# A four-block transformer kernel: the last stage's weights centred on the chip, and two engines' attention loops written out

## The reference

```python
def _layernorm(x, g, b):
    m = jnp.mean(x, axis=-1, keepdims=True)
    v = jnp.mean(jnp.square(x - m), axis=-1, keepdims=True)
    return (x - m) * jax.lax.rsqrt(v + LN_EPS) * g + b
...
gate_scores = xf @ gate_W + gate_b
topk_scores, topk_idx = jax.lax.top_k(gate_scores, 2)
weights = jax.nn.softmax(topk_scores, axis=-1)
def expert(w1, bb1, gg1, bbe1, w2, bb2, gg2, bbe2):
    h = jax.nn.relu(_layernorm(xf @ w1 + bb1, gg1, bbe1))
    return _layernorm(h @ w2 + bb2, gg2, bbe2)
...
out = jnp.sum(weights[..., None] * exp_out, axis=1)
return (out + xf).reshape(B, N, D)
```

## Time and profile before

| | us |
|---|---|
| median of 3 runs | 2317.06 |
| lowest and highest | 2315.38, 2320.44 |
| the profiled execution | 2316.81 |
| its span | 2315.0 |

### The profile page before, as it was taken

The page is one execution under the profiler, slowest core; times in us unless marked ns, Lnnn a source line. Parts: engine busy times, 40 slices in busy tenths (PEclk is TensorE's granted clock), DMA queues, the critical chain, the costliest instruction groups (busy, mean ns, idle before and its releaser), DMA issues.

```text
span 2315.0 us, 55192 instructions
## 1 busy us (share of the span) xinstructions
PE 2190.0 (95%) x18512; PEld 1811.2 (78%) x18512; DVE 1749.1 (76%) x4736; ACT 1193.1 (52%) x2397; POOL 1230.9 (53%) x2200
## 2 busy tenths in 40 slices
PE   6999999999699999999969999999989999999997
PEld 5878778777588888888858888888777777777775
DVE  5888888887465665666569887788678888888885
ACT  4655555555233333233236666666566666666663
POOL 5667667676200000000057666666468888888886
PEclk9999999999799999999989999999999999999998
DMA  7412121211221222221042222222100000000000
GB/s 233 143 58 65 56 65 57 63 59 49 103 94 40 91 84 85 86 83 55 28 135 66 75 69 68 73 66 71 49 26 29 28 28 27 27 27 27 27 24 17
DMA packets 125389, 148.06 MB, mean 64 GB/s; under 512 B 13835, under 2 KB 117523, under 8 KB 122773
## 3 DMA queue, kind: packets, MB, share of 16 engines
q1 hardware_dynamic: 119060, 128.84, 17.4%
q0 software_dynamic: 6144, 16.79, 2.3%
...
## 4 chain that ended last, share of the span: by engine, by line
PE 71%; DVE 11%; POOL 8%; issue 5%; ACT 2%; DMA 1%; POOLq 0%; SPq 0%; DVEq 0%; ACTq 0%
PE ps L1201 11%; PE ps L1074 10%; PE ps L1215 8%; PE ps L1059 5%; PE ps L1139 5%; PE ps L1217 4%; PE ps L1013 4%; PE ps L1158 4%; PE ps L972 4%; DVE u2g L1275 3%; PE ps L925 3%; PE ps L1106 3%; PE ps L1030 2%; DVE h_st L1244 2%; PE ps L1007 2%
## 5 line engine op out<-in xcount | busy, mean ns | idle before, releaser
L1344 DVE TENSOR_REDUCE nmax<-ps 128x16 f32<-128x2048 f32 x128 | 293.0, 2289 | 51.4 <-PE ps L1030 51.4
L665 POOL COPY slot_in<-slot_all 128x1 int32 (+1 forms) x64 | 18.2, 284 | 566.9 <-DMA eo_d<-eo 566.9
L896 ACT ACTIVATE hid<-ps,b_in 128x512 f32<-128x512 f32 x192 | 132.4, 690 | 361.0 <-PE ps L1201 338.4
L834 ACT ACTIVATE prob_t<-ps 128x2048 f32<-128x2048 f32 x128 | 240.5, 1879 | 76.6 <-PE ps L1013 76.6
L1215 PE MATMUL ps<-w_hl,hid_hi 128*128 128x512 f32 x768 | 269.6, 394 | 0.0
L1201 PE MATMUL ps<-xgt_hi,w_hl 128*128 128x512 f32 x768 | 242.9, 392 | 1.5 <-DVE xgt_lo L1543 1.5
L972 PE MATMUL ps<-w2f,a_t 128*128 128x256 f32 x1024 | 243.3, 381 | 0.0
L972 PEld LDWEIGHTS ps<-w2f,a_t 128*128 128x128 f32 x1024 | 195.5, 191 | 27.4
L1217 PE MATMUL ps<-w_hl,hid_lo 128*128 128x256 f32 x768 | 214.9, 280 | 0.0
L748 ACT ACTIVATE z<-ps,h_rs 128x256 f32<-128x256 f32 x256 | 123.7, 563 | 164.6 <-POOL h_rs L620 164.6
L639 POOL TENSOR_TENSOR km_r<-qk,cst 128x512 fp32r<-128x512 f32 x128 | 133.4, 1042 | 119.1 <-ACT qk L824 118.8
...
## 6 DMA issues: line engine op xcount, KB each, us to landing
c_t<-in_ctx_in_dram SPq DMA_DIRECT2D x128, 128.0 KB
...
x_d<-x SPq DMA_DIRECT2D x128, 128.0 KB, 2.1
...
```

The lines of the kernel that those rows point to most:

```text
L834: nc.scalar.activation(prob_t[:].rearrange("p a k -> p (a k)"), scores.rearrange("p a k -> p (a k)"), ACT.Exp, scale=SOFT).then_inc(y["exp ...
L896: nc.scalar.activation(hid[:, fc % 2, :], ps[:, 4 + fc % 2, 0:G], ACT.Gelu, bias=b1_in[:, e.parity, fc:fc + 1]).then_inc(z["hid_done"].sem, 1)
L1344: nc.vector.tensor_reduce(nmax[:, b.parity, :, 0:4], scores.rearrange("p a (r k) -> p a r k", k=P), AX_X, ALU.max, negate=True).then_inc(y ...
```

## The change

Each expert's w1, w2 and b2 are centred on the chip: the mean over the output columns is taken off each row of the weights and off the bias, so that the results of both matmuls have mean zero. The first and the second normalisation then need no mean. GpSimd drops the last two instructions of h_rs and the last of the k group, z is an ACT.Copy with a scale and no bias, gw8 and be_in keep four columns and four rows, and one load goes. The statistics are still taken. The means and subtractions are ten new large instructions on VectorE, and the preparation now runs from step 7 to step 42 of the second attention, with at most one large instruction of VectorE at the end of a step; ScalarE's parts move with it. Finally both attentions are written out on VectorE and on ScalarE (span None).

```diff
@@ GpSimd, fstep
                     nc.gpsimd.tensor_tensor(k_rw[:], k_rs[:, 1, :], gw8[:, b.parity, 0:E1], ALU.mult).then_inc(st.sem, 1)
-                    pool.wait_ge(st.of(b), st.at(b, 3))
-                    nc.gpsimd.tensor_tensor(gw8[:, b.parity, E1:2 * E1], k_mv[:, :, 0], k_rw[:], ALU.mult).then_inc(st.sem, 1)
...
                     nc.gpsimd.tensor_tensor(h_rs[:, 1, :], h_rs[:, 0, :], neg_half.to_broadcast([P, E1]), ALU.pow).then_inc(st.sem, 1)
-                    pool.wait_ge(st.of(b), st.at(b, 2))
-                    nc.gpsimd.tensor_tensor(h_rs[:, 2, :], h_mv[:, :, 0], h_rs[:, 1, :], ALU.mult).then_inc(st.sem, 1)
-                    pool.wait_ge(st.of(b), st.at(b, 3))
-                    nc.gpsimd.tensor_tensor(h_rs[:, 3, :], h_rs[:, 2, :], neg_one.to_broadcast([P, E1]), ALU.mult).then_inc(st.sem, 1)
@@ ScalarE, fstep
-                        nc.scalar.activation(z1[:, b.parity, e, :], ps[:, 2 + e // 2, (e % 2) * D:(e % 2 + 1) * D], ACT.Identity,
-                                             scale=h_rs[:, 1, e:e + 1], bias=h_rs[:, 3, e:e + 1]).then_inc(f["z_act"].sem, 1)
+                        nc.scalar.activation(z1[:, b.parity, e, :], ps[:, 2 + e // 2, (e % 2) * D:(e % 2 + 1) * D], ACT.Copy,
+                                             scale=h_rs[:, 1, e:e + 1]).then_inc(f["z_act"].sem, 1)
@@ ScalarE, preparation: w1_hi now at LAST_SPLIT + 12 and + 13
-                        nc.scalar.activation(b2_hi[:], b2_raw[:], ACT.Copy).then_inc(s_fset, 1)
+                    if n == 1 and s.off == LAST_SPLIT + 28:
+                        act.wait_ge(s_fset2, 20)
+                        nc.scalar.activation(b2_hi[:], b2_raw[:], ACT.Copy).then_inc(s_fset, 1)
-                run_steps(act, B, LEAD, TAIL[n], WARM, step, SPAN)
+                run_steps(act, B, LEAD, TAIL[n], WARM, step, None)
@@ VectorE, preparation
+                    if n == 1 and s.off == LAST_SPLIT + 3:
+                        dve.wait_ge(s_fset2, 1)
+                        nc.vector.tensor_reduce(w1_mean[:, 0], w1f[:, 0], AX_X, ALU.add).then_inc(s_fset2, 1)
...
+                    if n == 1 and s.off == LAST_SPLIT + 8:
+                        dve.wait_ge(s_fset2, 5)
+                        nc.vector.tensor_tensor(w1f[:, 0], w1f[:, 0], w1_mean[:, 0].unsqueeze(2).to_broadcast([P, E1, D]), ALU.subtract)\
+                            .then_inc(s_fset2, 1)
...
+                    if n == 1 and s.off == LAST_SPLIT + 23:
+                        dve.wait_ge(s_fset2, 17)
+                        nc.vector.tensor_tensor(w2f[:, 0:2], w2f[:, 0:2], w2_mean[:, 0:2].unsqueeze(3).to_broadcast([P, 2, C, D]), ALU.subtract)\
+                            .then_inc(s_fset2, 1)
...
-                run_steps(dve, B, LEAD, TAIL[n], WARM, step, SPAN)
+                run_steps(dve, B, LEAD, TAIL[n], WARM, step, None)
```

More of the change, by code:

```diff
@@ L324, in flamingo_gated @@
         b2_raw = psb("b2_raw", [2, E1, D])
+        w1_mean = psb("w1_mean", [P, C, E1])
+        w2_mean = psb("w2_mean", [P, E1, C])
+        b2_mean = psb("b2_mean", [2, E1])
         b2_hi = psb("b2_hi", [2, E1, D], F32R)
@@ L355, in flamingo_gated @@
         h_mv = psb("h_mv", [P, E1, 2])
-        h_rs = psb("h_rs", [P, 4, E1])
+        h_rs = psb("h_rs", [P, 2, E1])
         s_set = sem("s_set")
@@ L461, in layer1_weights @@
                     sp.dma_start(dst[0:E1] if dst is be2_in else dst[:], src).then_inc(s_fw, 16)
-                sp.dma_start(be2_in[E1:2 * E1], g2_1[0]).then_inc(s_fw, 16)
             def attention_weights(n):
@@ new lines, in step @@
+                    if n == 1 and s.off == LAST_SPLIT + 2:
+                        nc.vector.tensor_tensor(w1f[:, 1], w1f[:, 1], w1_first[:, 1], ALU.subtract).then_inc(s_fset2, 1)
+                    if n == 1 and s.off == LAST_SPLIT + 3:
+                        dve.wait_ge(s_fset2, 1)
+                        nc.vector.tensor_reduce(w1_mean[:, 0], w1f[:, 0], AX_X, ALU.add).then_inc(s_fset2, 1)
+                    if n == 1 and s.off == LAST_SPLIT + 4:
+                        dve.wait_ge(s_fset2, 2)
+                        nc.vector.tensor_reduce(w1_mean[:, 1], w1f[:, 1], AX_X, ALU.add).then_inc(s_fset2, 1)
@@ L1502, in step @@
+                    if n == 1 and s.off == LAST_SPLIT + 10:
+                        nc.vector.tensor_tensor(w1f[:, 1], w1f[:, 1], w1_mean[:, 1].unsqueeze(2).to_broadcast([P, E1, D]), ALU.subtract)\
+                            .then_inc(s_fset2, 1)
+                    if n == 1 and s.off == LAST_SPLIT + 14:
+                        dve.wait_ge(s_fset, 2)
                         nc.vector.tensor_tensor(w1_lo[:, 0], w1f[:, 0], w1_hi[:, 0], ALU.subtract).then_inc(s_fset2, 1)
-                    if n == 1 and s.known and s.off == LAST_SPLIT + 4:
-                        dve.wait_ge(s_fset, 5)
+                    if n == 1 and s.off == LAST_SPLIT + 15:
+                        dve.wait_ge(s_fset, 4)
@@ new lines, in step @@
+                    if n == 1 and s.off == LAST_SPLIT + 18:
+                        nc.vector.tensor_reduce(w2_mean[:, 2:4], w2f[:, 2:4], AX_X, ALU.add).then_inc(s_fset2, 1)
+                    if n == 1 and s.off == LAST_SPLIT + 20:
+                        nc.vector.tensor_reduce(b2_mean[:], b2_raw[:], AX_X, ALU.add).then_inc(s_fset2, 1)
+                    if n == 1 and s.off == LAST_SPLIT + 21:
+                        dve.wait_ge(s_fset2, 15)
+                        nc.vector.tensor_scalar(w2_mean[:], w2_mean[:], 1.0 / D, None, ALU.mult).then_inc(s_fset2, 1)
+                        nc.vector.tensor_scalar(b2_mean[:], b2_mean[:], 1.0 / D, None, ALU.mult).then_inc(s_fset2, 1)
@@ new lines, in step @@
+                    if n == 1 and s.off == LAST_SPLIT + 27:
+                        nc.vector.tensor_tensor(b2_raw[:], b2_raw[:], b2_mean[:].unsqueeze(2).to_broadcast([2, E1, D]), ALU.subtract)\
+                            .then_inc(s_fset2, 1)
+                    if n == 1 and s.off == LAST_SPLIT + 29:
+                        nc.vector.tensor_scalar(g2_in[:], g2_in[:], g_t[:, 3:4], None, ALU.mult).then_inc(s_fset2, 1)
+                    if n == 1 and s.off == LAST_SPLIT + 31:
+                        dve.wait_ge(s_fset, 5)
@@ L1508, in step @@
                         nc.vector.tensor_tensor(b2_lo[:], b2_raw[:], b2_hi[:], ALU.subtract).then_inc(s_fset2, 1)
-                        nc.vector.tensor_scalar(be2_in[0:2 * E1], be2_in[0:2 * E1], be_sign, None, ALU.mult).then_inc(s_fset2, 1)
-                    if n == 1 and s.known and s.off == LAST_SPLIT + 6:
-                        dve.wait_ge(s_fset2, 9)
+                    if n == 1 and s.off == LAST_SPLIT + 33:
+                        dve.wait_ge(s_fset2, 22)
                         nc.vector.tensor_scalar(b2_lo[:], b2_lo[:], hilo_mask[:, 1:2], None, ALU.mult).then_inc(s_fset2, 1)
```

58 lines of the change are left out of this document (30 added, 28 removed).

## The result

| | us (the ratio has no unit) |
|---|---|
| changed kernel, median of 4 runs | 2291.45 |
| lowest and highest | 2290.61, 2291.59 |
| its profiled execution, span | 2291.34, 2289.4 |
| the kernel before, in the same comparison | 2317.36 |
| ratio, 95% interval | 0.9885 (0.9872 to 0.9897) |

I forecast 2297.0 and a range of 2291 to 2304. Scaled to the median of 2317.06 that the forecast started from, the ratio gives 2290.4, just outside the range. The mechanism in the last stage was right and the gain was forecast too small. Medians and ratios in this document are over undisturbed runs; two runs of the kernel before beside e1 to e4, 2401.8 and 3554.6 us at granted clocks of 0.90 and 0.56, are left out.

A forecast was written before the change was run, and what follows sets the result against it. The prediction took a ring of waits across four engines in the last stage as the bound. Its gains, 17.1 + 2.2 + 0.3 + 0.2 = 19.8 us, off 2316.8 gave 2297.0 us, range 2291 to 2304.

The forecast's parts named there:

- The ring: Last stage: waits from k_st through k_rs, frs, xf and TensorE back to k_st set the round, 9.56 to 9.28 us.
- the wait for z at L991: Last stage: TensorE's 0.19 us wait for z, forecast to be gone after the change.
- 0.28 x 61 = 17.1: Last stage: the removed k instruction (L582) saves 0.28 us in each of 61 rounds, 17.1 us.
- Two thirds of what is removed is worth nothing.: Last stage: the first ring still decides at 9.28 us, so most of the removed GpSimd work gains nothing.
- the second ring: Last stage: waits through k_st, u2g, h_rs and z spanning two rounds, 19.1 us, falling to about 18.0, 9.0 a round.
- The ends: Last stage, where rounds fill and drain: a gain of 2.2 us, bounds 0.5 and 3.
- The centring: Second attention: ten new VectorE instructions, 12 us of work, taken as hidden at 0; up to 12 us if not.
- the split pair: Second attention: ScalarE's 1.5 us pair in one step (b2_hi and be2_in) is split up, gaining 0.3 us.
- The contention that the prediction weighed: Second attention: five two-input VectorE subtractions could hold up GpSimd's km_r and qm, and TensorE, by at most 6 us.
- The loops written out: Both attentions: 0 in the second, a gain of 0.2 us taken for the edit, bounds -1 and +3.
- The register instructions and the branch are therefore covered now: First attention: four steps take 34.78 us both written out and inside the loop, so loop overhead was taken as hidden.
- The clock: First attention: falls of the granted clock after TensorE's waits, about 1.3 us each; net change taken as 0.

The follow-up runs named there:

- e1: The changed kernel with VectorE's and ScalarE's loops of the first attention back; median 2295.11 us.
- e4: The changed kernel with a fourth GpSimd instruction of the k group back, its result unread; median 2314.21 us.
- e12: The changed kernel run once more, unchanged, in a second set of runs; median 2294.82 us.
- e8: The changed kernel with only ScalarE's loop of the first attention back; median 2295.29 us.
- e2: The kernel before with all attention loops of VectorE and ScalarE written out and nothing else changed; median 2316.11 us.
- e11: The changed kernel with only VectorE's loop of the first attention back; median 2297.09 us.

## Why the prediction was right, and where it was too small

**The ring.** Right in its place, its links and its end: 9.56 to 9.28 in written-out rounds, L954 0.05 us behind xf, the wait for z at L991 gone. The term 0.28 x 61 = 17.1 was mis-sized: it measured 19.5 (18.8 in e12's profile), because 40 of the 61 rounds are looped and lose 0.34. I had read the link in the written-out part and carried it over.

**"Two thirds of what is removed is worth nothing."** True of the kernel before: without the k group's part (e4) the h and z edits leave the round at 9.59, against 9.60. In the changed kernel they carry 0.12 us a round, because the second ring stood at 9.41 once the first was at 9.28. The prediction allowed for both, so its sum was right, but the sentence was not: of the 0.32 us, 0.20 comes with the k instruction and the last 0.12 needs both edits. A slip beside it: z's four instructions are 0.37 us by the rows and 0.33 in the sum of the second ring; they measured 0.36.

**The ends.** 2.2 us forecast. The first profile has 2.11 + 0.86 = 3.0, the upper bound; e12's has 0.55 + 0.76 = 1.3 (its stretches are 18.97 and 28.05 us). The forecast lies between them, but neither tests it. The first round alone takes 7.72 us in the first profile and 9.95 in e8's, and the stretch behind the last h_rs 26.4 in e1's and 29.3 in e8's, all with the same code in the last stage. What recurs is the second round: 9.99 us in the kernel before and in e2, 9.69 to 9.71 in the changed one.

**The centring.** Forecast 0 for the new work and a gain of 0.3 for the split pair. From the 4th nmax of the second attention, counted from 0, to the last it takes 447.82 us in every profile with the new preparation, give or take 0.02, and 448.23 in the kernel before and in e2. So the gain is 0.4 us. It fits the waits: the 0.4 us for v_aug of the earlier trace rows is gone in the changed kernel and in e12, the 0.6 is still there. The same comparison gives 0 for writing out this stage's loops, as forecast. The rest of the 1.08 us in the table lies in the first four steps and did not come again: e12's whole second attention takes 476.75 us.

The contention that the prediction weighed does show, on another instruction of GpSimd than the two that it named. slot_in stands beside a reduction (one tensor input) and beside a subtraction (two):

```profile
1253.94 1.21 DVE L1496 TENSOR_REDUCE w_mean<-w1f 128x4 f32<-128x1024 f32 x1
1254.08 0.18 POOL L661 COPY slot_in<-slot_all 128x1 int32<-128x1 int32 x1
...
1291.87 1.21 DVE L1507 TENSOR_TENSOR w1f<-w1f,w_mean 128x1024 f32<-128x1024 f32 x1
1292.00 1.14 POOL L661 COPY slot_in<-slot_all 128x1 int32 x1
```

0.18 us beside the reduction, 1.14 beside the subtraction, until 0.06 us behind its end. All five subtractions do this (1.11 to 1.14 us) and none of the five reductions. It delays GpSimd by some 0.95 us each time, and TensorE, which needs nothing of it so soon, doesn't wait.

**The loops written out.** This is the step that failed. "The register instructions and the branch are therefore covered now" rested on the earlier trace rows, and both pairs of rows there lie between two turns. Counted from 0, they are nmax 9 to 13, before the loop, and 33 to 37; the turns end at 24, 32, 40 and so on. The pair from 20 to 24, across a turn and undisturbed in that profile, takes 35.00 us, where e12 takes 34.64. The rule of the Trainium skill that I set aside (Runtime: NRT & Kernel Launch, Instruction fetch mechanics: a taken branch out of the fetched window stalls, straight code streams) agrees in sign with what e11 measures on VectorE, 0.23 to 0.38 us a turn. No run tells the fetch from the register instructions that go with a loop, so the cause of the stall is open. ScalarE's turn shows nothing in the time. The term was 1.7 us instead of 0.2.

**The clock.** I took 0 and gave each fall nearly its right price, 1.3 us for 1.45. The profile of before has five falls at 1.45 us, that of after three and a loss of 1.1 in its opening group: 7.2 against 5.4 us, so 1.8 of the 3.75 us in the first attention are this. By e12, 2294.8, the gain is 23.4 us, and the time lies inside the range.

So 19.8 became 25.6 by the spans: 2.4 by looped rounds, 1.5 by VectorE's loop, 0.8 at the ends, 1.8 by the clock, and 0.8 in the second attention (1.1, where I had 0.3). Against them stand 1.7 us at the start and in the experts, for which no cause is shown; 0.2 us of the first attention are left over. What comes again from profile to profile is 18.8 to 19.5 in the rounds, 1.7 by VectorE's loop, 0.4 in the second attention and 0.3 in the second round, 21 to 22 us. The two mis-sized terms, looped rounds and VectorE's loop, are why it is more than 19.8. What carried the first measurement past the range was luck on top: the clock, the first round and the first steps of the second attention.
